# A ring of four fp32 buffers for the GELU output in a two-block Swin kernel

## The chip, the cores and the metric

The kernel runs on one core of a Trainium2 chip. The metric is device time in microseconds (us) of one launch; the median of three runs is quoted. The profile is one further execution, taken by the hardware profiler.

## What is computed

The input is 32 images of 192 channels and 32x32 pixels, fp32. Two Swin blocks with their own weights follow one another; both compute, on tokens of 192 channels:

```
x = x + roll_back(proj(window_attention(roll(layernorm1(x)))))   # 8x8 windows, 12 heads of 16, shift 4
x = x + fc2(gelu(fc1(layernorm2(x))))                            # 192 -> 768 -> 192
```

The first block has a relative position bias and a shift mask in its softmax, the second has neither. The MLP, where the change lies, is `h = gelu(x @ w_fc1 + b_fc1)` with the exact GELU, then `h @ w_fc2 + b_fc2`.

## The kernel before

**Tiling.** A tile is 128 tokens (two windows), 8 tiles make an image, and with two blocks there are 512 visits of a tile. The order of the visits interleaves block 2 of one image with block 1 of a later one, in groups of four tiles. Every engine runs the same loop over slots `s`; a slot holds the attention work of one visit at several stages of a software pipeline. Each engine's instruction order in a slot is written out by hand, and the engines meet only through semaphores: `ge("gelu", u)` waits until the GELU number `u` is done, and so on.

**Precision.** fp32 values are multiplied as two fp16 parts, a high and a low one, so each product is three to five matmuls.

**The MLP phase.** The MLP runs on groups of four tiles (512 tokens), 128 phases in all, each spread over four slots, called place 0 to 3. The hidden layer has 768 channels, six chunks of 128, numbered `m` = 0 to 5 (`u` counts them over the whole run). A chunk passes these steps:

- PE, `hidden(m)`, line 588: five matmuls of 512 columns into `ps_s[:, u % 2]`, a PSUM ring of two banks. From `m` = 2 on it waits for `gelu(u - 2)`, which frees the bank.
- ACT, `gelu(m)`, line 716: reads the bank, writes fp32 into `hid[:, u % 2]`, a ring of two buffers in SBUF. It waits for `h_lo(u - 2)`, which frees the buffer.
- POOL, `hidden_hi(m)`, line 1130: rounds `hid` to fp16, the high part. It waits for `gelu(u)`.
- DVE, `hidden_lo(m)`, line 961: `hid` minus the high part, in fp16. It waits for `h_hi(u)`.
- PE, `mlp_out`, line 601: multiplies both parts by the fc2 weights, tile by tile; the first of them waits for `h_lo` of chunk 5.

The array `hid` is a view of `scaled`, a fp32 scratch of 3 x 768 columns used while the weights are prepared at the start.

**Where the chunks stand in each engine's order.** PE: `hidden(0)` to `hidden(3)` end place 0 (the `qk_product` of a later visit comes ahead of them), `hidden(4)` and `hidden(5)` begin place 1; then `x_transpose` (only if a later visit is of block 1), `rel_scores` (block 1 only) or not, `pv_product`, `v_product`, `scores`, `projection`, `p_transpose`, `shift_scores`, `qk_product`, and then `mlp_out`. At place 1 the scores wait for `gelu` of chunk 5, since they use the same PSUM banks. ACT: `exp`, the load of the GELU table, `gelu(0)`, `qk_hi`, `gelu(1)` at place 0; `gelu(2)`, `gelu(3)`, `norm2_hi`, `gelu(4)`, `gelu(5)` at place 1, then `v_hi` and the load of the exp table. POOL: `scale`, `apply1`, `apply2` and `hidden_hi(0)` to `(3)` at place 0; `norm1_lo` (line 1123), `hidden_hi(4)`, `norm2_lo` (line 1108), `set_mask` (line 1059), `hidden_hi(5)` at place 1. DVE: `p_lo`, `hidden_lo(0)`, `qk_lo`, `hidden_lo(1)`, `statistics` (line 881) at place 0; `hidden_lo(2)`, `hidden_lo(3)`, `mean_variance`, `inverse_sums`, `hidden_lo(4)`, `o_norm`, `row_max` (line 923), `attention_residual`, `statistics`, `v_lo`, `hidden_lo(5)` at place 1.

Of the kernel before, what the change touches and what calls it, by code (L numbers as in the profile page):

```python
# [40 lines left out]
ALU = mybir.AluOpType  # L41
ACT = mybir.ActivationFunctionType
# [7 lines left out]
TOK = 2 * WIN  # L50
# [3 lines left out]
GROUP = 4  # L54
# [31 lines left out]
def visit(n):  # L86

    image, layer, half = GROUPS[n // GROUP]
    return image, layer, half * GROUP + n % GROUP
# [20 lines left out]
def mlp_phase(s):  # L110

    return (s - LATE) // GROUP, (s - LATE) % GROUP
# [28 lines left out]
def swin_program(nc, x, layers, rel_bias, ident_in, q_mask_in, k_mask_in, out):  # L141
    H2 = C // 2
    with ExitStack() as ctx:
        def sb(name, shape, dt):
            return ctx.enter_context(nc.sbuf_tensor(name, shape, dt))
# [6 lines left out]
        ps_s = ctx.enter_context(nc.psum_tensor("ps_s", [128, 2, 512], F32))  # L152
# [12 lines left out]
        scaled = sb("scaled", [128, 3, HID], F32)  # L165
# [16 lines left out]
        b_fc1 = [sb(f"b_fc1{l}", [128, HC], F32) for l in range(LAYERS)]  # L182
# [28 lines left out]
        o_tok = sb("o_tok", [128, 2, C], F32)  # L211
        os = sb("os", [128, 2, 2, C], F16)
        ot = sb("ot", [128, 2, 3, TOK], F16)
        hid = scaled[:, :, :].rearrange("p a n -> p (a n)")[:, 0:2 * GROUP * TOK].rearrange("p (r t) -> p r t", r=2)
        hid16 = sb("hid16", [128, 2, HC, GROUP * TOK], F16)


# [25 lines left out]
        def when(eng, name, n):  # L243

            if n >= 0:
                eng.wait_ge(S[name], min(n + 1, COUNT[name]))
# [419 lines left out]
        def _(act):  # L666
# [3 lines left out]
            def slot(s):  # L670
                def ge(name, n):
                    when(act, name, n)
# [38 lines left out]
                def gelu(m):  # L711
                    _, layer, _ = visit(p * GROUP)
                    u = p * HC + m
                    ge("fc1", u)
                    ge("h_lo", u - 2)
                    nc.scalar.activation(hid[:, u % 2, :], ps_s[:, u % 2, :], ACT.Gelu, bias=b_fc1[layer][:, m:m + 1],  # L716
                                         scale=UNSCALE).then_inc(S["gelu"], 1)

                def load_exp():
# [21 lines left out]
                p, place = mlp_phase(s)  # L741
                mlp = 0 <= p < PHASES
                last_block = mlp and visit(p * GROUP)[1] == 1
                if mlp and place == 1:
                    gelu(2)
                    gelu(3)
                if live(s - 4):
                    norm2_hi(s - 4)
                if mlp and place == 1:
                    gelu(4)  # L750
                    gelu(5)
# [30 lines left out]
        def _(dve):  # L782
            v = nc.vector
# [84 lines left out]
            def slot(s):  # L868
                def ge(name, n):
                    when(dve, name, n)  # L870
# [86 lines left out]
                def hidden_lo(m):  # L957
                    u = p * HC + m
                    ge("gelu", u)
                    ge("h_hi", u)  # L960
                    v.tensor_tensor(hid16[:, 1, m, :], hid[:, u % 2, :], hid16[:, 0, m, :], ALU.subtract)\  # L961
                        .then_inc(S["h_lo"], 1)

                p, place = mlp_phase(s)
                mlp = 0 <= p < PHASES
                if mlp and place == 1:
                    hidden_lo(2)
                    hidden_lo(3)
# [4 lines left out]
                if mlp and place == 1:  # L973
                    hidden_lo(4)
# [34 lines left out]
        def _(pool):  # L1009
            g_ = nc.gpsimd  # L1010
# [38 lines left out]
            def slot(s):  # L1049
                def ge(name, n):  # L1050
                    when(pool, name, n)
# [74 lines left out]
                def hidden_hi(m):  # L1126
                    u = p * HC + m
                    ge("gelu", u)
                    pool.nop(nofuse=True)
                    g_.tensor_scalar(hid16[:, 0, m, :], hid[:, u % 2, :], 1.0, 0.0, ALU.mult, ALU.add)\  # L1130
                        .then_inc(S["h_hi"], 1)

                p, place = mlp_phase(s)
# [3 lines left out]
                if mlp and place == 1:  # L1137
                    hidden_hi(4)
# [4 lines left out]
                if mlp and place == 1:  # L1143
                    hidden_hi(5)
# [11 lines left out]
                if mlp and place == 0:  # L1156
                    for m in range(4):
                        hidden_hi(m)
# [57 lines left out]
```

## Time and profile before

| | |
|---|---|
| median of 3 runs | 4284.71 us (4282.59 to 4286.51) |
| profiled execution, its own time | 4277.42 us |
| its span | 4275.6 us |
| granted TensorE clock | 0.999 |
| PE busy | 3951.3 us (92%) |
| DVE busy | 3365.8 us (79%) |
| POOL busy | 3071.3 us (72%) |
| ACT busy | 2701.6 us (63%) |

Matmuls overlap in their pipeline, so PE's busy share is not its share of peak. "PEld" is PE's weight load, which runs ahead of the matmuls. Idle time in brackets stands before the instruction that it delayed, with the instruction whose end released it.

### The profile page before, as it was taken

Reading aid. Unit: us, or ns where it says so; the run is one execution under the profiler, and the core shown is the slowest. Engines: PE = TensorE matmul, PEld = TensorE weight load, DVE = VectorE, ACT = ScalarE, POOL = GpSimd, SP = SyncE. Lnnn points to the kernel's source line nnn. Section 1 sums busy time; section 2 is a strip of 40 time slices with the busy share of each in tenths; the row PEclk is TensorE's granted clock in tenths of the full one; section 3 lists DMA queues with packets and bytes.
Section 4 is the critical chain, followed back from the end, with each engine's and each line's share of the span. In section 5 each row is a group of like instructions: output and inputs, shape, how many; then the busy total and the mean of one; then the engine's idle time right before and its main releaser. Section 6 shows DMA issues by size and latency. Waiting matters only on the chain. (4 is left out here: it accounts for less than half of the span.)

```text
span 4275.6 us, 174432 instructions
## 1 busy us (share of the span) xinstructions
PE 3951.3 (92%) x65872; PEld 2860.2 (67%) x65872; DVE 3365.8 (79%) x9093; ACT 2701.6 (63%) x5921; POOL 3071.3 (72%) x6257
## 2 busy tenths in 40 slices
PE   3899999999999999999999999999999999999998
PEld 2666766666766676676676667666666666766665
DVE  5878878778787787887878788787778878877785
ACT  0666666666666666666666666666666666666665
POOL 4777777777777777777777777777777777777764
PEclk9999999999999999999999999999999999999999
DMA  3554544544555555554545545455554555544542
GB/s 97 109 92 99 104 98 97 102 103 94 103 101 96 102 101 98 100 101 102 97 100 102 95 100 102 100 97 101 102 94 102 101 98 97 102 104 94 94 96 62
DMA packets 1545149, 421.03 MB, mean 98 GB/s; under 512 B 1441782, under 2 KB 1542522, under 8 KB 1544316
## 3 DMA queue, kind: packets, MB, share of 16 engines
q1 hardware_dynamic: 1544316, 409.88, 49.6%
q8 instruction: 528, 8.65, 0.8%
q14 instruction: 305, 2.50, 0.2%
HBM read 32.15 MB, written 25.17 MB: 13 GB/s over the span
## 5 line engine op out<-in xcount | busy, mean ns | idle before, releaser
L588 PE MATMUL ps_s<-xh,w_fc 128*128 128x512 f16 x3840 | 909.6, 380 | 83.2 <-ACT stage L702 60.9
L961 DVE TENSOR_TENSOR hid<-scaled,hid 128x512 f16<-128x512 f32 x768 | 597.5, 778 | 450.1 <-POOL hid L1130 427.1
L601 PE MATMUL bank<-w_fc,hid 128*128 128x192 f16 x9216 | 846.4, 246 | 94.7 <-DVE hid L961 92.2
L1067 POOL TENSOR_TENSOR rstd<-vare,half 128x2 f32<-128x2 f32 x520 | 360.6, 693 | 786.0 <-DVE vare L901 786.0
L601 PEld LDWEIGHTS bank<-w_fc,hid 128*128 128x128 f16 x9216 | 762.5, 98 | 183.4 <-DVE v_blk L917 156.7
L588 PEld LDWEIGHTS ps_s<-xh,w_fc 128*128 128x128 f16 x3840 | 335.4, 97 | 643.3 <-ACT scaled L716 219.2
L1130 POOL TENSOR_SCALAR hid<-scaled 128x512 f16<-128x512 f32 x768 | 609.7, 794 | 180.5 <-ACT scaled L716 179.6
L716 ACT ACTIVATE scaled<-ps_s,b_fc 128x512 f32<-128x512 f32 x768 | 528.9, 689 | 310.6 <-DVE hid L961 308.6
L708 ACT ACTIVATE pt<-ps_t 128x768 f16<-128x768 f32 x512 | 415.0, 810 | 311.6 <-PE ps_t L545 304.3
L681 ACT ACTIVATE xs<-xn 128x192 f16<-128x192 f32 x512 | 184.8, 361 | 610.6 <-POOL xn L1074 610.6
L464 PE MATMUL bank<-w_qkv,xh 128*128 128x384 f16 x2560 | 501.7, 326 | 6.2 <-DMA xh<-xs 3.6
L923 DVE TENSOR_REDUCE smax<-ps_s 128x12 bf16<-128x768 f32 x512 | 488.0, 953 | 17.5 <-PE ps_s L525 2.4
L702 ACT ACTIVATE stage<-ps_s 128x768 f32<-128x768 f32 x512 | 416.6, 814 | 134.5 <-PE ps_s L534 134.5
L928 DVE TENSOR_TENSOR pt<-ps_t,pt 128x768 f16<-128x768 f32 x512 | 489.5, 956 | 12.2
L688 ACT ACTIVATE qk<-bank 128x384 f16<-128x384 f32 x1024 | 450.4, 502 | 10.7 <-PE bank L464 10.5
L545 PE MATMUL ps_t<-ident,stage 128*128 128x128 f32 x3072 | 419.5, 273 | 0.3 <-issue 0.3
L562 PEld LDWEIGHTS bank<-v_blk,pt 128*64 128x64 f16 x18432 | 333.0, 112 | 128.6 <-issue 95.7
L907 DVE SCALAR_TENSOR_TENSOR qk<-bank,qk 128x192 f16<-128x192 f32 x1024 | 315.4, 349 | 104.2 <-ACT qk L688 102.0
L562 PE MATMUL bank<-v_blk,pt 128*64 128x34 f16 x18432 | 383.5, 185 | 4.7 <-DVE pt L928 4.4
L697 ACT ACTIVATE v_blk<-bank 64x192 f16<-64x192 f32 x1024 | 330.6, 323 | 87.1 <-PE bank L497 81.0
L464 PEld LDWEIGHTS bank<-w_qkv,xh 128*128 128x128 f16 x2560 | 246.0, 97 | 179.7 <-DVE x_mid L948 6.1
L917 DVE SCALAR_TENSOR_TENSOR v_blk<-bank,v_blk 64x192 f16<-64x192 f32 x1024 | 357.4, 349 | 7.1
(113 smaller groups left out, 7133.2 us busy)
## 6 DMA issues: line engine op xcount, KB each, us to landing
x_img<-in_x_dram SPq DMA_DIRECT2D x256, 96.0 KB, 2.2
out_dram<-y_img SPq DMA_DIRECT2D x256, 96.0 KB, 1.9
xh<-xs SPq DMA_TRANSPOSE x520, 2.5
qkt<-qk SPq DMA_TRANSPOSE x512, 3.4
ot<-os SPq DMA_TRANSPOSE x512, 2.3
stage<-in_L_conv_fc_w_dram SPq DMA_DIRECT2D x2, 384.0 KB, 4.2
stage<-in_L_conv_w_fc_dram SPq DMA_DIRECT2D x2, 384.0 KB, 4.6
stage<-in_L_conv_qkv_w_dram SPq DMA_DIRECT2D x2, 288.0 KB
```

What stands on the lines that cost most here:

```text
L464: last = mm(dst, blocks[:, blk, :], w[:, part, n0:n1], start=(i == 0), stop=(i == 4 and bias is None))
L545: last = nc.tensor.transpose(ps_t[:, g // 3, (g % 3) * TOK:(g % 3 + 1) * TOK], p_tok[:, n % 2, g].rearrange("p a k -> p (a k)"), ident[:, :])
L562: last = mm(ps_o[rows, g * 2 * VW:(g + 1) * 2 * VW].rearrange("p (a d) -> p a d", a=2), pt[:, n % 2, ps, g, rows], v_blk[:, n % 2, vs, :, ...
L588: last = mm(ps_s[:, u % 2, :].rearrange("p (a t) -> p a t", a=GROUP), w_fc1[layer][:, part, m * 128:(m + 1) * 128], xh[:, p % 2 * GROUP:(p ...
L601: mm(bank[:, 0:C], hid16[:, hs, m, tok], w_fc2[layer][:, ws, m, :], start=(m == 0 and i == 0), stop=False)
L688: last = copy(qk[:, n % QK, i * HEADS:(i + 1) * HEADS, places, :], src.broadcast_to([128, HEADS, 2, HD]), ACT.Copy, scale=UNSCALE)
L702: nc.scalar.activation(p_tok[:, n % 2].rearrange("p g a k -> p a g k"), ps_s[:, :, 0:PAIRS * WIN].rearrange("p a (g k) -> p a g k", g=PAIR ...
L716: nc.scalar.activation(hid[:, u % 2, :], ps_s[:, u % 2, :], ACT.Gelu, bias=b_fc1[layer][:, m:m + 1], scale=UNSCALE).then_inc(S["gelu"], 1)
L923: v.tensor_reduce(smax[:, n % 2], ps_s[:, :, 0:PAIRS * WIN].rearrange("p a (g k) -> p a g k", g=PAIRS), AX.X, ALU.max).then_inc(S["max_don ...
L928: v.tensor_tensor(pt[:, n % 2, 1].rearrange("p (b g) t -> p b (g t)", b=2), ps_t[:, :, 0:3 * TOK], pt[:, n % 2, 0].rearrange("p (b g) t -> ...
L961: v.tensor_tensor(hid16[:, 1, m, :], hid[:, u % 2, :], hid16[:, 0, m, :], ALU.subtract)\
L1130: g_.tensor_scalar(hid16[:, 0, m, :], hid[:, u % 2, :], 1.0, 0.0, ALU.mult, ALU.add)\
```

## The change

The view `hid` gets four buffers of 512 columns instead of two, in the same scratch (2048 of its 2304 columns). The three places that index it take `u % 4`, and `gelu(m)` waits for `h_lo(u - 4)` instead of `h_lo(u - 2)`. The PSUM ring `ps_s` keeps its two banks, and no instruction is added, removed or moved.

```
-        hid = scaled[:, :, :].rearrange("p a n -> p (a n)")[:, 0:2 * GROUP * TOK].rearrange("p (r t) -> p r t", r=2)
+        hid = scaled[:, :, :].rearrange("p a n -> p (a n)")[:, 0:4 * GROUP * TOK].rearrange("p (r t) -> p r t", r=4)
...
-                    ge("h_lo", u - 2)
-                    nc.scalar.activation(hid[:, u % 2, :], ps_s[:, u % 2, :], ACT.Gelu, bias=b_fc1[layer][:, m:m + 1],
+                    ge("h_lo", u - 4)
+                    nc.scalar.activation(hid[:, u % 4, :], ps_s[:, u % 2, :], ACT.Gelu, bias=b_fc1[layer][:, m:m + 1],
...
-                    v.tensor_tensor(hid16[:, 1, m, :], hid[:, u % 2, :], hid16[:, 0, m, :], ALU.subtract)\
+                    v.tensor_tensor(hid16[:, 1, m, :], hid[:, u % 4, :], hid16[:, 0, m, :], ALU.subtract)\
...
-                    g_.tensor_scalar(hid16[:, 0, m, :], hid[:, u % 2, :], 1.0, 0.0, ALU.mult, ALU.add)\
+                    g_.tensor_scalar(hid16[:, 0, m, :], hid[:, u % 4, :], 1.0, 0.0, ALU.mult, ALU.add)\
```

## Rows read from the trace of the kernel before

**Rows 1.** The page, part 1: busy us (share of the span) and instructions.

```profile
PE 3951.3 (92%) x65872; PEld 2860.2 (67%) x65872; DVE 3365.8 (79%) x9093; ACT 2701.6 (63%) x5921; POOL 3071.3 (72%) x6257
```

**Rows 2.** Waits: who waited <- for whom: us in total, times, longest us.

```profile
DVE hid L961 <- POOL hid L1130: 427.1, 504, 3.2
ACT scaled L716 <- DVE hid L961: 308.6, 510, 1.4
PEld ps_s L588 <- ACT scaled L716: 219.2, 510, 1.3
...
PE bank L601 <- DVE hid L961: 92.2, 128, 2.9
```

**Rows 3.** Timeline of one phase, PE and ACT: start us, us, instruction [idle before].

```profile
2025.77 7.19 PE L588 MATMUL ps_s<-xh,w_fc 128*128 128x512 f16 x30 [0.55 <-ACT stage L702]
...
2028.37 0.70 ACT L716 ACTIVATE scaled<-ps_s,b_fc 128x512 f32<-128x512 f32 x1
...
2029.12 0.76 PEld L588 LDWEIGHTS ps_s<-xh,w_fc 128*128 128x128 f16 x5 [0.45 <-ACT scaled L716]
...
2029.68 0.69 ACT L716 ACTIVATE scaled<-ps_s,b_fc 128x512 f32<-128x512 f32 x1 [0.61 <-DVE hid L961]
...
2030.42 0.76 PEld L588 LDWEIGHTS ps_s<-xh,w_fc 128*128 128x128 f16 x5 [0.54 <-ACT scaled L716]
...
2030.95 0.69 ACT L716 ACTIVATE scaled<-ps_s,b_fc 128x512 f32<-128x512 f32 x1 [0.59 <-DVE hid L961]
...
2033.76 0.69 ACT L716 ACTIVATE scaled<-ps_s,b_fc 128x512 f32<-128x512 f32 x1 [0.85 <-DVE hid L961]
```

**Rows 4.** Timeline, PE alone, in two narrow windows of that phase.

```profile
2029.12 1.04 PE L588 MATMUL ps_s<-xh,w_fc 128*128 128x512 f16 x4
...
2030.42 0.39 PE L588 MATMUL ps_s<-xh,w_fc 128*128 128x512 f16 x1
```

**Rows 5.** Timeline of that phase, POOL and DVE.

```profile
2028.17 0.62 POOL L1130 TENSOR_SCALAR hid<-scaled 128x512 f16<-128x512 f32 x1
...
2028.90 0.69 DVE L961 TENSOR_TENSOR hid<-scaled,hid 128x512 f16<-128x512 f32 x1 [2.24 <-POOL hid L1130]
...
2029.22 0.84 POOL L1130 TENSOR_SCALAR hid<-scaled 128x512 f16<-128x512 f32 x1 [0.43 <-ACT scaled L716]
...
2030.17 0.69 DVE L961 TENSOR_TENSOR hid<-scaled,hid 128x512 f16<-128x512 f32 x1
...
2030.52 0.81 POOL L1130 TENSOR_SCALAR hid<-scaled 128x512 f16<-128x512 f32 x1 [0.46 <-ACT scaled L716]
...
2030.78 0.35 DVE L881 BATCH_NORM_STATS2 bn<-x_new 128x6 f32<-128x192 f32 x1
...
2032.58 0.54 POOL L1123 TENSOR_TENSOR xs<-xn,xs 128x191 f16<-128x191 f32 x1
...
2032.71 0.96 DVE L961 TENSOR_TENSOR hid<-scaled,hid 128x512 f16<-128x512 f32 x1 [0.58 <-POOL hid L1130]
...
2033.09 1.05 POOL L1130 TENSOR_SCALAR hid<-scaled 128x512 f16<-128x512 f32 x1
...
2034.12 0.54 POOL L1108 TENSOR_TENSOR xs<-xn,xs 128x192 f16<-128x192 f32 x1
...
2034.25 0.96 DVE L961 TENSOR_TENSOR hid<-scaled,hid 128x512 f16<-128x512 f32 x1 [0.18 <-POOL hid L1130]
...
2034.63 0.67 POOL L1059 TENSOR_SCALAR qk<-k_mask 128x48 f16<-128x48 f32 x1
```

**Rows 6.** Timeline of that phase, from the scores to the MLP output.

```profile
2034.59 0.38 PE L525 MATMUL ps_s<-qkt 64*64 64x64 f16 x24 [0.36 <-ACT scaled L716]
...
2035.40 0.94 DVE L923 TENSOR_REDUCE smax<-ps_s 128x12 bf16<-128x768 f32 x1
...
2037.66 0.69 DVE L961 TENSOR_TENSOR hid<-scaled,hid 128x512 f16<-128x512 f32 x1
...
2038.50 1.65 PE L601 MATMUL bank<-w_fc,hid 128*128 128x192 f16 x18 [0.79 <-DVE hid L961]
```

## Prediction, made before the run

> **What bounds the kernel now.** I read the page first, then the waits, then the timeline of one MLP phase. PE is busy 92% of the span [rows 1], so outside the start of the program it is PE's idle time that a change of this kind can win. The waits show a loop [rows 2]: ACT waits 510 times (four of six chunks, 128 phases) for `hidden_lo` to free a buffer, 308.6 us; PE's weight loads wait 510 times for a GELU to free a bank; DVE waits for `hidden_hi` 504 times; and once in each phase PE's first `mlp_out` matmul waits for `hidden_lo`, 92.2 us in all.
>
> The timeline shows the loop at work [rows 3]. One chunk is five matmuls. Their starts lie (1.04 - 0.39)/3 = 0.217 us apart and one lasts 0.39 us [rows 4], so a chunk needs 1.08 us of PE. But from chunk 2 on the GELUs start every 1.27 us (2029.68, 2030.95), each released by DVE, and PE's weight loads follow each GELU's end: 2030.42 instead of 2029.12 + 1.08 = 2030.20. The last GELU starts only at 2033.76.
>
> The second thing the timeline shows is that `hidden_hi` on POOL and `hidden_lo` on DVE do not run side by side [rows 5]. `hidden_hi(0)`, alone, takes 0.62 us. `hidden_hi(1)` starts at 2029.22 inside `hidden_lo(0)`, which ends at 2029.59, and ends at 2030.06: 0.47 after that. `hidden_hi(2)` ends at 2031.33, again 0.47 after `hidden_lo(1)`. The same holds the other way: `hidden_lo` alone takes 0.69, but `hidden_lo(3)`, started inside `norm1_lo` (end 2033.12), ends 0.55 after it at 2033.67, and `hidden_lo(4)` ends 0.55 after `norm2_lo` (2034.66), at 2035.21. `hidden_hi(4)` ends 0.47 after `hidden_lo(3)`; `set_mask`, 2034.63 to 2035.30, ends 0.09 after `hidden_lo(4)`. So whoever starts second stands still until the first is done, and then needs its free duration less 0.14.
>
> Which of these ends last? After the hidden chunks the chain is: `hidden_hi(4)`, `hidden_lo(4)`, `o_norm`, `row_max` at 2035.40, the residual, statistics, `v_lo`, `hidden_lo(5)` at 2037.66, and then `mlp_out` at 2038.50, for which PE had waited 0.79 us [rows 6]. DVE has no gap from `hidden_lo(4)` to `hidden_lo(5)`. So what counts is how much sooner `hidden_lo(4)` ends. PE's own stalls ahead of the scores (0.36 us there) are not additional: they are won back only to be spent in front of `mlp_out`.
>
> **The change, step by step.** Nothing is added on any engine, and no DMA or queue is passed. What goes is the wait for `h_lo(u - 2)`. The wait for `h_lo(u - 4)` comes too early to hold: `hidden_lo(0)` ends at 2029.59, long before `gelu(4)`; `hidden_lo(1)` ends, below, at 2031.23, `gelu(5)` starts at 2032.56. Index arithmetic costs nothing, it is done when the program is built.
>
> PE and ACT. `hidden(3)` waits for the end of `gelu(1)` (2029.07), not touched by the ring: it stays at 2029.12. Chunk 2 follows chunks 0 and 1 without a gap, so its last matmul starts at 2025.77 + 14 x 0.216 = 2028.79 and ends at 2029.17; `gelu(2)` starts about 0.04 later, at 2029.21 instead of 2029.68, and ends at 2029.90. Chunk 3 ends at 2029.12 + 4 x 0.216 + 0.38 = 2030.37: `gelu(3)` 2030.41 to 2031.10 (was 2030.95). `hidden(4)` starts at 2030.20, and `gelu(4)` at 2031.49, ending 2032.18, with 0.39 us for `norm2_hi` between. `hidden(5)` starts at 2031.28, `gelu(5)` at 2032.56 (was 2033.76). PE is through with the hidden chunks at 2032.36, 0.42 us earlier than now (the row of 30 matmuls ends at 2032.96, of which 0.17 lies in the pipeline beside the next one).
>
> POOL and DVE. I take the 0.15 us from a GELU's end to `hidden_hi` and the 0.11 us from `hidden_hi`'s end to `hidden_lo` from [rows 3, 5] (2029.07 to 2029.22; 2028.79 to 2028.90), and let the two exclude each other as above:
>
> - `hidden_hi(2)`: GELU ready 2029.90 + 0.15, POOL free 2030.06. It starts before `hidden_lo(1)` (2030.17) and so runs free: ends 2030.68.
> - `hidden_lo(1)`: held until 2030.68, ends 2031.23 (now 2030.86, so this one gets later).
> - `hidden_hi(3)`: 2031.10 + 0.15 = 2031.25, free, ends 2031.87.
> - `hidden_lo(2)`: behind `statistics` (0.35 us), starts about 2031.5, held until 2031.87, ends 2032.42.
> - `norm1_lo`: held until 2032.42, ends 0.54 - 0.14 = 0.40 later, 2032.82.
> - `hidden_lo(3)`: held until 2032.82, ends 2033.37 (now 2033.67).
> - `hidden_hi(4)`: its GELU is long ready; held until 2033.37, ends 2033.84 (now 2034.14).
> - `norm2_lo`: starts at once, ends 2034.37; `hidden_lo(4)` starts at 2033.95, held, ends 2034.92 (now 2035.21).
>
> The gain is 2035.21 - 2034.92 = 0.29 us in a phase. `inverse_sums`, which stands between `hidden_lo(3)` and `(4)`, waits for `pv_product`, which comes 0.42 us earlier with PE; the scores need no wait for `gelu(5)` any more and are done before `row_max` wants them. From there DVE's gapless chain carries the 0.29 us to `mlp_out`. All later places hang on PE, DVE and POOL of this phase, so the next one begins 0.29 us sooner.
>
> The bounds of that term: none (0) if the shift is lost behind something else, and 0.56 us if the two engines did not exclude each other: then `hidden_hi(3)` would keep its present 0.81 us and run 2031.25 to 2032.06, with `norm1_lo` and `hidden_hi(4)` at their present 0.54 and 1.05 behind it, and `hidden_lo(4)` would start 0.55 earlier. I take 0.29, since every one of the seven overlaps I looked at obeys the exclusion to 0.01 us.
>
> Sum: 128 phases x 0.29 = 37 us. From the profiled execution, 4277.4 - 37 = 4240.4. It was 7.3 us under the median of the runs shown, so on their scale 4284.7 - 37 = 4247.6; I predict 4247.
>
> The Trainium skill, page "SBUF — State Buffer", section "SBUF: two separate sides", says that GpSimd and a VectorE instruction with two SBUF inputs share one port pair by an exclusive lock, and that whoever starts first holds it for its whole instruction. The trace agrees (0.47 and 0.55 us after the release), and it is this rule that speaks against the change: with it the sum is 37 us, without it 128 x 0.55 = 70 us.
>
> **Rivals.**
>
> *The exclusion binds less than I think* (chance 0.12). POOL's queue moves up by the full 0.55 us by which `gelu(3)` comes sooner (2030.95 to 2030.41). For it: today POOL waits for the GELU before each `hidden_hi` (0.46 us [rows 5]). Against it: counted from 2028.90, `hidden_lo(0)` to `(3)`, `hidden_hi(1)` to `(4)` and `norm1_lo` fill 4.94 us with hardly a gap in my schedule. Time: 4284.7 - 70 = 4214.
>
> *The gain is given back* (0.16). PE arrives at `mlp_out` or at a later wait no sooner, because something not moved by the phase (the transposing DMAs, the pipeline of a later slot) ends last. For it: PE idles in small pieces elsewhere too. Against it: every later row depends on rows moved here, and the wait before `mlp_out` is 92.2 us in total. Time: between 4270 and 4285.
>
> *POOL wins every handover* (0.08, the other side). Place: when `hidden_hi(3)` ends at 2031.87 both `hidden_lo(2)`, waiting since 2031.5, and `norm1_lo`, started at 2031.83, want to go. If POOL keeps its turn, there and at every later handover, as soon as its queue is full (it is, since the GELUs now run ahead), then `norm1_lo` ends at 2032.27, `hidden_lo(2)` 2032.82, `hidden_hi(4)` 2033.29, `norm2_lo` 2033.69, `set_mask` 2033.78, `hidden_hi(5)` 2034.25, and only then `hidden_lo(3)` 2034.80. `inverse_sums` and `hidden_lo(4)` follow to about 2035.9, 0.7 us later than today: 128 x 0.7 = 90 us, 4375 us. It decides from the point where DVE loses two handovers in a row. Against it: in the trace `hidden_hi(4)` was started (2033.09) just before `norm1_lo` ended, and `hidden_lo(3)`, waiting, was served first, in this phase as in the others I read.
>
> **How the numbers follow.** Forecast 0.64, the rivals 0.12, 0.16 and 0.08. The forecast's own spread is 4235 to 4262 (0.38 to 0.18 us a phase). The range for 8 in 10 takes in the first rival and part of the second: 4212 to 4274. A measurement of this kernel can tell about 0.2%, 8.6 us, from no change. Faster by more: 0.64 + 0.12 + 0.05 = 0.81. Within: 0.10, most of the second rival. Slower: 0.09, the third and what I have not thought of.
>
> **What the profile after would show.** Right: ACT waits for `hidden_lo` almost never; the GELUs 2 to 5 start 1.08 to 1.28 us apart and the last one some 6.8 us after the first hidden matmul, not 8.0; `hidden_lo(1)` lengthens from 0.69 to about 1.05; `hidden_lo(4)` ends 9.15 us after that matmul, not 9.44; the scores start without idle; and PE's wait before `mlp_out` grows, to about 1 us or moves to the wait for `row_max`, since PE gains more ahead of it than DVE does. Wrong: `mlp_out` not 0.3 us closer to the first hidden matmul; POOL or DVE rows that overlap at their free durations; or `hidden_lo(2)` or `(3)` longer than 1.2 us, which is the third rival.

## The result, and the profile after

The changed kernel takes 4240.21 us (median of 5 runs, 4235.41 to 4241.64) against 4284.71 us (here five runs too, with the same median): ratio 0.9894, 95% interval 0.988 to 0.9909, 44.5 us less. Its profiled execution has a span of 4233.6 us, 42.0 less than before. Forecast were 37 us less and 4247 us.

The page after, part 1. Against [rows 1], PE's busy time falls by 41.4 us, since the hidden matmuls of a phase now overlap without stalls (line 588 alone: 909.6 to 866.5 us). DVE's rises by 65.8 us, though it has no more work: `hidden_lo` takes 896 instead of 778 ns in the mean, and the time for which POOL holds it counts as busy.

```profile
PE 3909.9 (92%) x65872; PEld 2873.0 (68%) x65872; DVE 3431.6 (81%) x9093; ACT 2718.3 (64%) x5921; POOL 3081.7 (73%) x6257
...
L961 DVE TENSOR_TENSOR hid<-scaled,hid 128x512 f16<-128x512 f32 x768 | 678.1, 896 | 347.3 <-POOL hid L1130 327.4
```

The waits after. ACT's wait for `hidden_lo` [rows 2] is gone from the list; ACT now waits for PE. The wait of PE's weight loads for a GELU falls from 219.2 to 108.0 us. PE's wait before `mlp_out` grows a little, from 92.2 to 104.7 us, and its wait for `row_max` (L923) in front of `shift_scores` (L534) grows from 10.8 us in 57 waits to 62.1 in 129: PE is early there now.

```profile
ACT scaled L716 <- PE ps_s L588: 121.0, 261, 1.7
...
PEld ps_s L588 <- ACT scaled L716: 108.0, 385, 1.3
PE bank L601 <- DVE hid L961: 104.7, 128, 2.6
...
PE ps_s L534 <- DVE smax L923: 62.1, 129, 1.1
```

The timeline after of a phase of the same kind as in [rows 3, 5, 6]; a row with x2 is two instructions in one, and the last row is cut off by the end of the window.

```profile
2008.89 6.77 PE L588 MATMUL ps_s<-xh,w_fc 128*128 128x512 f16 x30 [0.55 <-ACT stage L702]
...
2011.50 1.52 ACT L716 ACTIVATE scaled<-ps_s,b_fc 128x512 f32<-128x512 f32 x2
...
2012.35 1.43 POOL L1130 TENSOR_SCALAR hid<-scaled 128x512 f16<-128x512 f32 x2 [0.43 <-ACT scaled L716]
...
2013.30 1.02 DVE L961 TENSOR_TENSOR hid<-scaled,hid 128x512 f16<-128x512 f32 x1
...
2014.52 1.98 DVE L961 TENSOR_TENSOR hid<-scaled,hid 128x512 f16<-128x512 f32 x2
...
2014.97 0.98 POOL L1123 TENSOR_TENSOR xs<-xn,xs 128x191 f16<-128x191 f32 x1
...
2015.70 0.69 ACT L716 ACTIVATE scaled<-ps_s,b_fc 128x512 f32<-128x512 f32 x1 [0.39 <-PE ps_s L588]
...
2015.92 1.05 POOL L1130 TENSOR_SCALAR hid<-scaled 128x512 f16<-128x512 f32 x1
...
2016.88 0.38 PE L525 MATMUL ps_s<-qkt 64*64 64x64 f16 x24
2016.94 0.55 POOL L1108 TENSOR_TENSOR xs<-xn,xs 128x192 f16<-128x192 f32 x1
...
2017.08 0.95 DVE L961 TENSOR_TENSOR hid<-scaled,hid 128x512 f16<-128x512 f32 x1 [0.29 <-POOL hid L1130]
...
2018.22 0.94 DVE L923 TENSOR_REDUCE smax<-ps_s 128x12 bf16<-128x768 f32 x1
...
2019.22 0.50 PE L534 MATMUL ps_s<-smax,neg_ident 128*128 128x384 bf16 x2 [0.71 <-DVE smax L923]
...
2020.48 0.69 DVE L961 TENSOR_TENSOR hid<-scaled,hid 128x512 f16<-128x512 f32 x1
...
2021.32 1.31 PE L601 MATMUL bank<-w_fc,hid 128*128 128x192 f16 x14 [0.78 <-DVE hid L961]
```

Count from the first hidden matmul, 2008.89. The last GELU starts at 6.81 (before: 7.99), PE's scores at 7.99 without idle (8.82), `hidden_hi(4)` ends at 8.08 (8.37), `hidden_lo(4)` at 9.14 (9.44), `row_max` starts at 9.33 (9.63) and `mlp_out` at 12.43 (12.73). ACT is 1.18 us ahead of where it was and PE 0.83 us, and only 0.30 us of it arrives at `mlp_out`.

What follows `mlp_out` is unchanged. Two windows show it, first of the kernel before and then of this one: the stretch to `mlp_out`, and from there to the next phase. Columns: length, then busy time and count of PE, PEld, DVE, ACT and POOL, the granted clock, the DMA engines' busy share and GB/s.

```profile
2025.77:2038.50 12.73, 11.35 (x132) 5.93 (x133) 9.16 (x19) 10.27 (x19) 9.37 (x15) 1.00 0.28 62
2038.50:2057.94 19.44, 18.89 (x382) 16.26 (x382) 16.61 (x52) 10.93 (x31) 14.90 (x36) 1.00 0.66 121
```

```profile
2008.89:2021.32 12.43, 10.94 (x132) 6.06 (x132) 9.70 (x19) 10.79 (x20) 9.40 (x15) 1.00 0.28 63
2021.32:2040.76 19.44, 18.89 (x382) 16.26 (x383) 16.61 (x52) 10.55 (x30) 14.93 (x36) 1.00 0.65 121
```

Over all 128 phases the first stretch has a mean of 12.73 us before and 12.40 after, and the second 19.56 and 19.55; 0.33 + 0.01 us over 127 steps is 43 us, about the difference of the spans (42.0).

### The profile page after: what moved, and what is told of

It is laid out like the page before. It is cut to its first block and busy times, and to the rows that moved or that the text cites. A ratio compares the mean times of both kernels' runs of the same rounds, so it can differ in the third digit from the quotient of the medians.

```text
span 4233.6 us, 174430 instructions
## 1 busy us (share of the span) xinstructions
PE 3909.9 (92%) x65872; PEld 2873.0 (68%) x65872; DVE 3431.6 (81%) x9093; ACT 2718.3 (64%) x5921; POOL 3081.7 (73%) x6257
## 5 line engine op out<-in xcount | busy, mean ns | idle before, releaser
L961 DVE TENSOR_TENSOR hid<-scaled,hid 128x512 f16<-128x512 f32 x768 | 678.1, 896 | 347.3 <-POOL hid L1130 327.4
L601 PE MATMUL bank<-w_fc,hid 128*128 128x192 f16 x9216 | 846.1, 246 | 106.3 <-DVE hid L961 104.7
L588 PE MATMUL ps_s<-xh,w_fc 128*128 128x512 f16 x3840 | 866.5, 379 | 70.6 <-ACT stage L702 62.9
L588 PEld LDWEIGHTS ps_s<-xh,w_fc 128*128 128x128 f16 x3840 | 355.5, 97 | 567.5 <-issue 112.4
L1130 POOL TENSOR_SCALAR hid<-scaled 128x512 f16<-128x512 f32 x768 | 562.7, 738 | 131.8 <-ACT scaled L716 130.6
L923 DVE TENSOR_REDUCE smax<-ps_s 128x12 bf16<-128x768 f32 x512 | 488.1, 953 | 16.2 <-PE ps_s L525 1.3
L928 DVE TENSOR_TENSOR pt<-ps_t,pt 128x768 f16<-128x768 f32 x512 | 489.6, 956 | 12.2
L907 DVE SCALAR_TENSOR_TENSOR qk<-bank,qk 128x192 f16<-128x192 f32 x1024 | 315.6, 350 | 103.1 <-ACT qk L688 100.7
```

The lines of the kernel that those rows point to most:

```text
L588: last = mm(ps_s[:, u % 2, :].rearrange("p (a t) -> p a t", a=GROUP), w_fc1[layer][:, part, m * 128:(m + 1) * 128], xh[:, p % 2 * GROUP:(p ...
L601: mm(bank[:, 0:C], hid16[:, hs, m, tok], w_fc2[layer][:, ws, m, :], start=(m == 0 and i == 0), stop=False)
L923: v.tensor_reduce(smax[:, n % 2], ps_s[:, :, 0:PAIRS * WIN].rearrange("p a (g k) -> p a g k", g=PAIRS), AX.X, ALU.max).then_inc(S["max_don ...
L928: v.tensor_tensor(pt[:, n % 2, 1].rearrange("p (b g) t -> p b (g t)", b=2), ps_t[:, :, 0:3 * TOK], pt[:, n % 2, 0].rearrange("p (b g) t -> ...
L961: v.tensor_tensor(hid16[:, 1, m, :], hid[:, u % 4, :], hid16[:, 0, m, :], ALU.subtract)\
L1130: g_.tensor_scalar(hid16[:, 0, m, :], hid[:, u % 4, :], 1.0, 0.0, ALU.mult, ALU.add)\
```

## The experiments

Each ratio is to the kernel before, timed on the same chip. Experiments 1 to 4, 5 to 7 and 8 were timed apart, and the kernel before had a median of 4284.3, 4281.0 and 4283.5 us beside them; where two such groups are compared, the difference by the ratios is given too.

**1. Three buffers (`ring3`).**

```
-        hid = scaled[:, :, :].rearrange("p a n -> p (a n)")[:, 0:4 * GROUP * TOK].rearrange("p (r t) -> p r t", r=4)
+        hid = scaled[:, :, :].rearrange("p a n -> p (a n)")[:, 0:3 * GROUP * TOK].rearrange("p (r t) -> p r t", r=3)
...
-                    ge("h_lo", u - 4)
+                    ge("h_lo", u - 3)
```

All three places index it with `u % 3`.

> Three buffers instead of four, and gelu(u) waits for h_lo(u - 3). My theory: the gain comes only from the GELUs not waiting for hidden_lo of two chunks before; with the exclusion between DVE and POOL, hidden_lo(1) ends 5.46 us and hidden_lo(2) 6.65 us after the first hidden matmul, while gelu(4) starts at 5.73 and gelu(5) at 6.80, so a third buffer is enough by about 0.15 us: 4240 us, ratio 0.989 to the kernel before, the same as with four. Rival (each further buffer brings its share of the gain): half of it, about 4262 us.

Measured: 4237.5 us, ratio 0.9888 (0.9874 to 0.9903). The third buffer brings all of it; the fourth brings nothing that the runs can tell.

**2. Four buffers with the old wait (`ring4_old_wait`).**

```
-                    ge("h_lo", u - 4)
+                    ge("h_lo", u - 2)
```

> Four buffers, but gelu(u) still waits for h_lo(u - 2). My theory: where the data lie is nothing, the wait is all: 4285 us, ratio 1.000 within 0.002. Rival (the two engines disturb one another less on four buffers, a matter of addresses): some of the 44 us are kept, ratio 0.990 to 0.996.

Measured: 4285.1 us, ratio 0.9997 (0.9988 to 1.0007). ACT's wait is back as it was:

```profile
ACT scaled L716 <- DVE hid L961: 310.7, 510, 1.4
```

So the gain is the wait's and not the addresses'.

**3. More work for PE (`pe_extra4`).**

```
-                    for g in range(PAIRS):
+                    for g in list(range(PAIRS)) + [2, 3, 4, 5] * (mlp and place == 1):
                         last = nc.tensor.transpose(...
```

> The changed kernel with four more 128-column fp32 transposes on PE at place 1 (the same data written again to the same bank), 0.44 us of PE a phase ahead of shift_scores. My theory: DVE's chain from hidden_lo(4) on bounds the phase, PE stands 0.2 to 0.7 us before shift_scores and 0.8 us before mlp_out, so this costs 0 to 10 us: 4240 to 4250 us. Rival (what the change saved was PE's time, 0.42 us of stalls in the hidden chunks, at 92% busy PE is the bound): 128 x 0.44 = 56 us more, 4296 us.

Measured: 4237.6 us, ratio 0.9891 (0.9874 to 0.9907): 0.43 us more of PE in every phase cost nothing. Its timeline shows ten transposes instead of six (0.82 us), and the wait for `row_max` behind them 0.28 us instead of 0.71:

```profile
2014.94 1.25 PE L545 MATMUL ps_t<-ident,stage 128*128 128x128 f32 x10
2016.47 0.50 PE L534 MATMUL ps_s<-smax,neg_ident 128*128 128x384 bf16 x2 [0.28 <-DVE smax L923]
```

PE, busy 92% of the span, is not the bound in this stretch.

**4. The exclusion of DVE and POOL (`norm2_late`).** At place 1 POOL no longer starts `norm2_lo` in the 0.1 us between `hidden_hi(4)` and `hidden_lo(4)`.

```
-                if live(s - 4):
+                if live(s - 4) and place != 1:
                     norm2_lo(s - 4)
                 if live(s + 3):
                     set_mask(s + 3)
+                if live(s - 4) and place == 1:
+                    norm2_lo(s - 4)
```

> The changed kernel with POOL's norm2_lo at place 1 moved behind set_mask, so that it no longer starts between hidden_hi(4) and hidden_lo(4). My theory (DVE and POOL exclude each other, and hidden_lo(4) is on the path): hidden_lo(4) ends at 8.84 instead of 9.14 us after the first hidden matmul, and all that follows comes 0.3 us sooner in each of 128 phases: 38 us less, 4202 us. Rival (no exclusion that matters; POOL's own order after hidden_hi(4) is off the path): 4240 us, no change. A second rival: norm2_lo's later end (by 0.6 us) delays the transposing DMA and gives the gain back: 4230 to 4245 us.

Measured: 4208.8 us, ratio 0.9822 (0.9808 to 0.9837), 31 us less than the changed kernel. One phase of its timeline, first hidden matmul at 2059.09:

```profile
2067.14 0.23 POOL L1059 TENSOR_SCALAR qk<-k_mask 128x48 f16<-128x48 f32 x1
2067.28 0.69 DVE L961 TENSOR_TENSOR hid<-scaled,hid 128x512 f16<-128x512 f32 x1 [0.30 <-POOL hid L1130]
2067.33 1.05 POOL L1108 TENSOR_TENSOR xs<-xn,xs 128x192 f16<-128x192 f32 x1
```

The roles are exchanged: `hidden_lo(4)` takes its free 0.69 us and ends at 8.88 (9.14 with the new ring alone), and `norm2_lo` takes 1.05 instead of 0.55 and ends 0.41 after it. In this phase `mlp_out` starts at 12.17 instead of 12.43. That is so in 90 of the 128 phases; in the other 38 it starts at about 12.27. In 30 of them `hidden_lo(5)`, now sooner, is itself held by POOL, by the copies of line 1014 that order a later tile, and takes 0.80 us instead of 0.69. The mean falls from 12.40 to 12.17, 29 us over 128 phases, which is the difference of the profiled spans. I had expected 0.30 a phase, having taken `hidden_lo(4)` to end at 8.84; nothing is given back behind `mlp_out` (the later stretch stays at 19.56).

**5. `norm1_lo` later too (`norm12_late`).** On top of experiment 4, at place 1 POOL's `norm1_lo` (line 1123) goes from ahead of `hidden_hi(4)` to behind it.

> norm2_late, and POOL's norm1_lo at place 1 behind hidden_hi(4) too. My theory: norm1_lo's 0.40 us leaves the queue for the shared access ahead of hidden_lo(3) and hidden_hi(4), but part comes back ahead of hidden_lo(4), which must also wait for inverse_sums (pv_product ends 7.5 to 7.6 us after the first hidden matmul): hidden_lo(4) ends at 8.63 to 8.72 instead of 8.84, 13 to 26 us less than norm2_late, 4183 to 4196 us. Rival (norm1_lo's later end delays the transposing DMA of a later slot and qk_product): 4209 us or more.

Measured: 4189.0 us, ratio 0.9787 (0.977 to 0.9803), 20 us less than `norm2_late` (15 by the ratios). `mlp_out` starts at 12.07. In a phase whose first hidden matmul is at 2049.89, `hidden_lo(4)` ends at 8.79, a little behind my range:

```profile
2057.55 0.23 DVE L934 RECIPROCAL o_inv<-bank 128x12 f32<-128x12 f32 x1 [0.32 <-PE bank L562]
2057.59 0.55 POOL L1123 TENSOR_TENSOR xs<-xn,xs 128x191 f16<-128x191 f32 x1
2057.72 0.96 DVE L961 TENSOR_TENSOR hid<-scaled,hid 128x512 f16<-128x512 f32 x1
```

`inverse_sums` (L934) now waits 0.32 us for `pv_product`, but it is not what ends last. The place that `norm2_lo` had left is taken by `norm1_lo`: it starts 0.13 us before `hidden_lo(4)` and holds it, so that it ends 0.54 us after `norm1_lo` and takes 0.96 us instead of 0.69. In the whole trace this is so in 125 of the 128 phases. By my estimate `hidden_lo(4)` would end 0.27 us sooner with `norm1_lo` behind `set_mask` too; no run tried it, and whether that would arrive at `mlp_out` is not shown.

**6. A sooner `hidden_lo(5)` (`stats_late`).** DVE's `statistics(s - 3, 1)` goes at place 1 from behind `attention_residual` to behind `hidden_lo(5)`.

> The changed kernel with DVE's statistics(s - 3, 1), 0.36 us, moved at place 1 from behind attention_residual to behind hidden_lo(5), so that v_lo and hidden_lo(5) come 0.36 us sooner but DVE's work to the end of the slot is the same. My theory: DVE's whole chain, not the moment of hidden_lo(5), sets the pace: mlp_out starts 0.36 us sooner, but p_lo, qk_lo and mlp_residual(0) do not, and v_product at place 2 then waits for mlp_residual(0): 4230 to 4240 us. Rival (PE's 0.79 us wait before mlp_out is what costs, so what shortens it is a gain): 128 x 0.36 = 46 us less, 4194 us.

Measured: 4218.8 us, ratio 0.9854 (0.984 to 0.9869), 21 us less than the changed kernel (17 by the ratios): neither. `mlp_out` starts 0.38 us sooner in most phases (0.36 in the mean), but the stretch after it has two kinds. With `x_transpose` and `rel_scores` on PE at place 2 it stays at 19.76 us; without them it grows from 19.44 to 19.81. A phase of the second kind shows why:

```profile
2014.31 0.96 DVE L928 TENSOR_TENSOR pt<-ps_t,pt 128x768 f16<-128x768 f32 x1
2015.38 0.68 PEld L562 LDWEIGHTS bank<-v_blk,pt 128*64 128x64 f16 x36 [0.37 <-issue]
2015.41 0.75 PE L562 MATMUL bank<-v_blk,pt 128*64 128x34 f16 x36 [0.17 <-DVE pt L928]
2015.71 0.35 DVE L948 SCALAR_TENSOR_TENSOR x_tok<-bank,x_tok 128x192 f32<-128x192 f32 x1
2016.11 0.28 PE L497 MATMUL bank<-w_qkv,xh 128*64 128x96 f16 x4
```

PE waits for `p_lo` (L928) at `pv_product`, and `v_product` (L497) starts right behind `mlp_residual(0)` (L948, end 2016.06). In the first kind PE has 0.8 us of other work there, and the stretch is no longer than before. My theory held in half the phases and was too strict in the other half.

**7. Experiments 5 and 6 together (`norm12_stats_late`).**

> norm12_late and stats_late together. My theory: the same as norm12_late within 10 us. Rival: the sum of both moves, some 46 us less than norm12_late.

Measured: 4170.6 us, ratio 0.9742 (0.9728 to 0.9757), 18 us less than `norm12_late`: the same half gain as in experiment 6, so more than my 10 us and less than half of 46.

**8. The norm's small operations further back, on top of experiment 5.** `centre_after_plo` puts `statistics`, `mean_variance` and `centre` behind `p_lo` at place 1, `centre_last` behind `mlp_residual(0)`; at their old places they are left out at place 1. The edit of `centre_after_plo`:

```
                 if live(s - 1):
                     p_lo(s - 1)
+                if place == 1:
+                    if live(s - 3):
+                        statistics(s - 3, 1)
+                        mean_variance(s - 3, 1)
+                    if live(s + 5) or live(s - 3):
+                        centre(s + 5)
```

> norm12_late, and at place 1 DVE's statistics, mean_variance and centre of the second norm go behind mlp_residual(0), so that hidden_lo(5) comes 0.36 us sooner and p_lo, qk_lo and mlp_residual(0) come 0.87 us sooner. norm12_stats_late showed that an earlier mlp_out alone is passed on only in the phases in which PE has other work before pv_product. My theory: with p_lo and mlp_residual(0) earlier too it is passed on in both kinds: 128 x 0.37 = 47 us less than norm12_late, 4142 us. Rival: rstd and the norms on POOL, and the transposes that SP issues behind them, come some 2 us later and end last: 4170 us or more.

> The same three operations only behind p_lo, so that p_lo comes 0.87 us sooner but qk_lo and mlp_residual(0) are where they were. Theory A (in the phases that passed nothing on, PE waits for p_lo only): 4142 us, as centre_last. Theory B (v_product waits for mlp_residual(0) right behind it): no more than norm12_stats_late, 4165 to 4172 us.

Measured: `centre_after_plo` 4165.4 us, ratio 0.9723 (0.9706 to 0.9739), theory B; 63 waits of `v_product` for `mlp_residual` are in its trace (13.1 us). `centre_last` 4237.8 us, ratio 0.9892 (0.9877 to 0.9906): 49 us more than `norm12_late` (45 by the ratios) where I had expected 47 less. `mlp_out` did start sooner (11.66 us instead of 12.04 in the mean), but the later stretch grew from 19.55 to 20.25 us, and the two together are 40 us over 127 steps. Its waits have entries that the kernel before has not, or hardly (3.5 us for the second, 0.6 for the third):

```profile
PEld bank L610 <- ACT y_img L738: 64.3, 62, 1.4
...
PE bank L610 <- DVE x_tok L948: 45.4, 68, 1.0
...
PE bank L464 <- DMA ot<-os: 27.2, 37, 2.3
```

PE itself waits for `mlp_residual` (L948) and for the transposing DMA of `ot`, which comes late, as the rival had it for the norms' transposes; which of the entries starts the delay stays open. The other 10 us lie ahead of the first hidden matmul (157.8 us after the start instead of 147.6). There PE stands still for 2.30 us up to 122.01, waiting for `ot`, and the granted clock is 0.50, its lower level of 1.2 GHz, from 121.1 to 127.9 us. It is so again from 145.0 to 151.8, after PE was busy for 0.45 of 2 us; in `norm12_late` it is 1.00 in both stretches. How much of the 10 us is the clock's was not separated.

## Why the prediction was right

**The loop.** Right. ACT waited 510 times for `hidden_lo`, now never by the list of waits, and experiment 2 brings the wait and the time back together. That `h_lo(u - 4)` comes too early to hold was right with room: `h_lo(u - 3)` holds only 9 times, 2.6 us in all.

**PE and ACT.** Right to some hundredths: the last GELU at 6.81 us (forecast 6.79), PE through 0.42 us earlier (the row of 30 matmuls 6.77 us long instead of 7.19). Experiment 3 shows that this gain was not the one that counts.

**The exclusion.** Right, and it is the step that the size hung on. The order forecast came out: `hidden_hi(2)` ran free, and `hidden_lo(1)` was held and took 1.02 us instead of 0.69 (forecast about 1.05); `norm1_lo` took 0.98 (0.99 worked out). `hidden_lo(4)` ended 0.30 us sooner (forecast 0.29). What the change would have brought without the exclusion is not shown. The 0.55 us and 70 us of the prediction are no clean sum of it: they keep durations that the exclusion itself makes longer (`hidden_hi(4)` with 1.05 us, 0.62 when free). Experiment 4 shows the exclusion from the other side: POOL's order alone, with no instruction more or less, moved `hidden_lo(4)` by 0.26 us and the time by 31 us. The Trainium skill ("SBUF — State Buffer", "SBUF: two separate sides") calls the shared access an exclusive lock whose loser fully blocks; the trace agrees, but a part of about 0.14 us of the blocked instruction is spent while it waits.

**The rest of the path.** The shift came through from `hidden_lo(4)` to `mlp_out` and to the next phase. Where I was not exact is in the sum, which is short: 37 us against 44.5 measured, and the interval of the ratio is 39 to 51 us. Most phases shrink by 0.30 or 0.31 us (32.49 to 32.18, 32.17 to 31.87), 39 us in all, and the spans differ by 42. The rest lies in single phases that take longer than their kind, of which the profile before has more than the one after, and in the spread of the runs (4 us from lowest to highest for the kernel before); no experiment was made on them.

**The rivals.** Of the three, none came. The exclusion did not bind less: `hidden_lo(4)` ended at 9.14 us, where 0.55 us sooner would have been 8.89. The gain was not given back; experiment 6 shows that it would have been in half of the phases, had only `mlp_out` and not DVE's whole chain moved. POOL did not win the handover at `hidden_hi(3)`'s end: `hidden_lo(2)`, waiting, went first, as read in the trace before. The 90 us of this rival were also too few. Its chain takes 0.14 us off POOL instructions that follow one another on POOL itself, while in [rows 5] `norm2_lo` ends 0.52 us after `hidden_hi(4)`, nearly its whole 0.55. With such steps the chain ends some 0.35 us later, by my estimate.

**Signs.** The scores without idle, the wait moved to `row_max`, 9.14 and 12.43 us: as written. Only the wait before `mlp_out` did not grow to 1 us but stayed at 0.78, since `row_max` holds PE back before it; this was the other branch of what I had written (0.71 us there in the phase shown, 0.16 in the phase before).

## What to carry to other kernels

A ring is deep enough when the wait for its oldest buffer never ends last. Here that was three buffers, and a fourth brought nothing; the timeline tells the number, by when the oldest buffer comes free and when its writer is otherwise ready. What a removed wait is worth is read where the engines next meet, at the one that comes last: here 0.30 us arrived of the 1.2 us by which the last GELU came sooner. Where two engines hold one another up, their durations are not constants: write down who starts first, and look whether an instruction off the path (here `norm2_lo`) starts just before one on it. After such a move look again, since another can take its place, as `norm1_lo` did in experiment 5. Moving two instructions of POOL and one of DVE took the kernel from 4240 to 4171 us (65 us less by the ratios); moving DVE's small operations too far back (`centre_last`) left it at 4238.

## What the runs showed of the hardware

DVE's `tensor_tensor` on two SBUF inputs (`hidden_lo`) and POOL's instructions on SBUF do not run beside each other. In the traces before and after, the one that started second ended after the first by its own free duration less about 0.14 us (0.55 of 0.69, 0.47 of 0.62, 0.41 of 0.55, 0.09 of 0.23); over the whole trace before, `hidden_hi` was second 511 times, and ended 0.48 us after `hidden_lo` in the median. Where the overlap was shorter than those 0.14 us, nothing was lost: in experiment 4 `hidden_lo(4)` started 0.09 us before `set_mask` ended and took its 0.69 us. DVE instructions that read one input from PSUM, or have only one, were not held: `qk_lo` (L907) took 0.35 us in the median beside POOL's instructions (852 times in the trace before) and in the 6 without them, and `statistics` (L881) 0.35 and 0.36.

At a handover the side that had been waiting went first, even when the other had its next instruction started a few hundredths of a microsecond before the release (`hidden_lo(3)` before `hidden_hi(4)` in [rows 5], `hidden_lo(2)` before `norm1_lo` in the timeline after). POOL's order alone was worth 31 us in this kernel (experiment 4).
